# One kernel, four places reordered: split stores, key weights and their loads, the routed experts' first tiles, and the turning of the queries' rows

## The reference

```python
x = x + mlstm(layernorm(x), ctx, ctx)          # 16 heads of 32, gates, decay matrix, normalised per head
x = x + moe(layernorm(x))                      # rms norm, 8 experts, top 2, silu(gate) * up, down; + a shared expert
x = x + xattn(layernorm(x), ctx)               # q, ki, vi: 16 heads of 128, q and k rms-normalised over 2048 columns
x = x + x @ ternary(weight).T + bias
# xattn, cut:
k_img = rms_norm(img_ctx @ ki_w + ki_b, nki_s) # ki_w 512 x 2048
v_img = img_ctx @ vi_w + vi_b
out = (softmax(q @ k_img.T / sqrt(128)) @ v_img) @ o_w + o_b
```

## Time and profile before

| | us |
|---|---|
| median of 3 runs (1359.07 to 1367.22) | 1366.83 |
| the profiled execution | 1370.19 |
| its span in the profile | 1368.5 |
| values and gates | 0 to 197 |
| heads and keys | 197 to 475 |
| routed experts | 569 to 781 |
| queries | 781 to 1003 |

### The profile page before, as it was taken

One profiled execution on the slowest core, in us unless ns is written; L12 is line 12 of the kernel. 1 busy time (PEld: TensorE's weight loads), 2 busy tenths in 40 slices (PEclk: granted clock), 3 DMA queues, 4 the chain that ended last, 5 costly groups with the idle time before them and its releaser, 6 DMA issues. The chain is left out here.

```text
span 1368.5 us, 24512 instructions
## 1 busy us (share of the span) xinstructions
PE 1298.8 (95%) x7390; PEld 1072.4 (78%) x7391; DVE 840.9 (61%) x1614; ACT 742.9 (54%) x1839; POOL 382.6 (28%) x358
## 2 busy tenths in 40 slices
PE   7998998989999899899989989999989999999998
PEld 6786876767776768688876678888878888888887
DVE  3644546767679774444444377635477777777865
ACT  4334538786777351345455545544676555556651
POOL 0111014273719006399331153036000000000041
PEclk9999999999999899999999999999999999999999
DMA  7847799877787194675648787473565555555403
GB/s 250 307 186 266 265 319 311 267 252 244 258 254 231 63 333 183 204 218 156 201 147 269 265 256 214 137 232 132 185 202 161 162 158 165 159 168 155 122 32 123
DMA packets 168183, 280.99 MB, mean 205 GB/s; under 512 B 29920, under 2 KB 58336, under 8 KB 167840
## 3 DMA queue, kind: packets, MB, share of 16 engines
q1 hardware_dynamic: 142288, 224.44, 51.6%
q0 software_dynamic: 8672, 29.37, 6.6%
q10 hardware_dynamic: 17136, 26.09, 5.2%
HBM read 171.04 MB, written 108.80 MB: 204 GB/s over the span
## 5 line engine op out<-in xcount | busy, mean ns | idle before, releaser
L120 PE MATMUL banks<-of_shared_split,key_lead 128*128 128x512 f32 x256 | 110.0, 430 | 17.5 <-DVE key_trail L1392 10.7
L2973 ACT ACTIVATE prob<-banks,attend_row,rq 128x128 f32<-128x128 f32 x248 | 110.4, 470 | 0.0
L2986 ACT ACTIVATE attend_ol<-banks,of_attend_vbias 128x512 fp32r<-128x512 f32 x64 | 44.2, 691 | 116.9 <-PE banks L3185 116.9
L120 PE MATMUL banks<-wo,attend_ol 128*128 (+1 forms) x256 | 106.3, 415 | 0.0
L121 PE MATMUL banks<-of_shared_split,key_lead 128*128 128x512 f32 x256 | 104.9, 410 | 0.0
L122 PE MATMUL banks<-of_shared_split,key_trail 128*128 128x512 f32 x256 | 104.8, 410 | 0.0
L120 PE MATMUL banks<-queries_rows_split,queries_wl 128*128 128x512 f32 x256 | 100.9, 394 | 0.0
L122 PE MATMUL banks<-wo,attend_ot 128*128 (+1 forms) x256 | 100.8, 394 | 0.0
L121 PE MATMUL banks<-wo,attend_ol 128*128 (+1 forms) x256 | 100.0, 391 | 0.0
L122 PE MATMUL banks<-queries_rows_split,queries_wt 128*128 128x512 f32 x256 | 99.9, 390 | 0.0
L121 PE MATMUL banks<-queries_rows_split,queries_wl 128*128 128x512 f32 x256 | 99.8, 390 | 0.0
(11 more groups left out here) (399 smaller groups left out, 3569.5 us busy)
## 6 DMA issues: line engine op xcount, KB each, us to landing
mlstm_gmax<-running_max SPq DMA_DIRECT2D x36, 512.0 KB, 5.8
k_heads<-heads_key ACTq DMA_DIRECT2D x64, 256.0 KB, 4.5
q_heads<-queries_head SPq DMA_DIRECT2D x64, 256.0 KB, 2.7
q_ahead<-q_heads SPq DMA_DIRECT2D x64, 256.0 KB, 4.2
of_attend_k<-k_heads SPq DMA_DIRECT2D x60, 256.0 KB, 4.0
of_attend_v<-v_heads SPq DMA_DIRECT2D x60, 256.0 KB, 3.3
key_raw<-in_L_xattn_ki_w SPq DMA_DIRECT2D x20, 512.0 KB, 5.4
sorted_rows<-of_shared_split SPq DMA_DIRECT2D x2, 5120.0 KB, 28.6
```

The lines of the kernel that those rows point to most:

```text
L120: nc.tensor.matmul(out, lead_l, lead_r, start=first, stop=False)
L2973: ins = nc.scalar.activation(prob[:, j % 2, b, :], ps[:, j % 2, b * S:(b + 1) * S], ACT.Exp, bias=row[:, j % 2, 1, b:b + 1], scale=rq[:, b ...
L2986: nc.scalar.activation(ol[:, par, j, :], ps[:, 4 + j % 2, :], ACT.Identity, bias=vbias[:, bass.ds(quad_of(it) * 4 + j, 1)]).then_inc(ol_do ...
```

## The change

In values and gates, the eight stores of the split context are issued at units 21, 22, 25 and 26 instead of 30, 32, 34 and 36, and the load of the third quarter of x comes at unit 8, behind a store of values, instead of 7.

In heads and keys, the inner pairs of `KEYS` alternate between groups for each head rather than each pair of heads; the weights of a visit are formed one unit earlier where its predecessor in the same buffer allows it (`SPLIT_AT`, `FORMED`); SyncE issues the eight split loads ahead of the other work of its step; and the tail's instructions are put in another order on ScalarE and VectorE.

In routed experts, the leads and trails of the second tile precede the cut of the second expert's weights, and the inputs of the first two down products are split ahead of the last gate.

In queries, `staged` counts batches, and TensorE turns the first group batch by batch.

```diff
--- before.py
+++ after.py
@@ -194,7 +194,8 @@
         TRAILS = {OPENS[q + 1] - (6 if q < QUADS - 2 else 5) + c: (q + 1, c) for q in range(QUADS - 1) for c in range(C)}
         STATS, NORMS = 8, 16
         GATES = [20 + (UNITS - 13 - 20) // 3 * g for g in range(G)]
-        TOKENS = {4: 0, 5: 1, 7: 2, 9: 3}
+        TOKENS = {4: 0, 5: 1, 8: 2, 9: 3}
+        SPLITS = {21: 0, 22: 1, 25: 2, 26: 3}
         TURN = len(FOURS) % 2
         AHEAD_AT = (OPENS[-2] + 2, OPENS[-2] + 4)
         stage = [A.kT[:].rearrange("p c n -> p (c n)").rearrange("p (b d) -> p b d", b=GB), A.ctx[:]]
@@ -291,11 +292,11 @@
                 if u % 4 == 0 and u:
                     store_four(u // 4 - 1)
                 if u in TOKENS:
-                    if u > 4:
+                    if u % 4:
                         sp.wait_ge(product, u - 1)
                     load_x(TOKENS[u])
-                if u % 2 == 0 and 30 <= u < 30 + 2 * G:
-                    g = (u - 30) // 2
+                if u in SPLITS:
+                    g = SPLITS[u]
                     sp.wait_ge(trail_done, (g + 1) * C)
                     for k, t in ((0, lead), (1, trail)):
                         sp.dma_start(split_dram[k, :, :, g * N:(g + 1) * N].rearrange("c p t -> p c t"),
@@ -712,11 +713,16 @@
     UNITS = PER * G
     HALF = PER // 2
     KEYS = [(k % 2 * HALF + 2 * p + j, g, k * HALF + 2 * p + j)
-            for k in range(G + 1) for p in range(HALF // 2) for g in (k - 1, k) if 0 <= g < G for j in range(2)]
+            for k in range(G + 1) for p in range(HALF // 2)
+            for g, j in ([(g, j) for g in (k - 1, k) for j in range(2)] if p in (0, HALF // 2 - 1) else
+                         [(g, j) for j in range(2) for g in (k - 1, k)]) if 0 <= g < G]
     VISITS = HALF * (G + 1)
     KEY_BANKS = (6, 7, 1)
     FIRST_OF = [min(u for u, key in enumerate(KEYS) if key[2] == v) for v in range(VISITS)]
     LAST_OF = [max(u for u, key in enumerate(KEYS) if key[2] == v) for v in range(VISITS)]
+    SPLIT_AT = [0, 0] + [max(LAST_OF[v - 2] + 2, FIRST_OF[v] - 1) for v in range(2, VISITS)]
+    FORMED = dict((SPLIT_AT[v], v) for v in range(2, VISITS))
+    assert len(FORMED) == VISITS - 2
     OPENS = [min(u for u, key in enumerate(KEYS) if key[1] == g) for g in range(G)]
     CLOSES = [max(u for u, key in enumerate(KEYS) if key[1] == g) for g in range(G)]
     with Phase(nc, "heads") as ph:
@@ -825,13 +831,17 @@
 
             def next_raw(g, m):
                 u = unit_number(g, m)
-                v = KEYS[u][2]
-                if u == FIRST_OF[v] and v % 2 and v // 2 + 2 < VISITS // 2:
+                v = FORMED[u] if u in FORMED else u if u < 2 else 0
+                if v % 2 and v // 2 + 2 < VISITS // 2:
                     sp.wait_ge(wt_done, v + 1)
                     A.load_raw(sp, (v // 2 + 2) % (PER // 2))
 
             def body(g, first, last=False):
                 for n in range(PER):
+                    if not first and not last and n == PER - 2 - LAG:
+                        sp.wait_ge(product, CLOSES[g - 1] + 1)
+                        for part in range(2 * C):
+                            A.load_split(sp, g + 1, part)
                     if n % 2 == 0:
                         k = n // 2
                         sp.wait_ge(dec_done, g * PER + n + 2)
@@ -858,10 +868,6 @@
                         load_ctx(g + 2, n - PER + GB)
                     if first and LAG <= n < LAG + 2 * C:
                         A.load_split(sp, 1, n - LAG)
-                    if not first and not last and n == PER - 2 - LAG:
-                        sp.wait_ge(product, CLOSES[g - 1] + 1)
-                        for part in range(2 * C):
-                            A.load_split(sp, g + 1, part)
                     if n == LAG and last:
                         sp.wait_ge(A.v_stored, 16 * ((H1 // 4 * G - len(DEFERRED)) // 2))
                         for w, at in zip(E1.weights, (0, C * F, 2 * C * F)):
@@ -1028,10 +1034,10 @@
 
             def weight_lead(g, m):
                 u = unit_number(g, m)
-                v = KEYS[u][2]
-                if u == FIRST_OF[v] and v >= 2:
+                if u in FORMED:
+                    v = FORMED[u]
                     act.wait_ge(product, LAST_OF[v - 2] + 1)
-                    A.weight_lead(act, KEYS[u][0], v // 4)
+                    A.weight_lead(act, KEYS[FIRST_OF[v]][0], v // 4)
 
             def keep_key(g, m):
                 u = unit_number(g, m)
@@ -1072,12 +1078,14 @@
             for g in range(1, G):
                 body(g, False)
             last = G - 1
-            row_sums(last)
             for m in range(PER - LAG, PER + 1):
-                if m + 1 < PER:
+                if m < PER - LAG + 2:
                     weight_lead(last, m + 1)
                 keep_key(last, m - 1)
+                if m == PER - LAG:
+                    row_sums(last)
                 if m == PER - LAG + 1:
+                    weight_lead(last, m + 2)
                     square(last, 0)
                     square(last, 1)
                     act.wait_ge(early_agg, 1)
@@ -1176,9 +1184,9 @@
 
             def weight_trail(g, m):
                 u = unit_number(g, m)
-                v = KEYS[u][2]
-                if v >= 2 and u == FIRST_OF[v]:
-                    A.weight_trail(dve, v, KEYS[u][0])
+                if u in FORMED:
+                    v = FORMED[u]
+                    A.weight_trail(dve, v, KEYS[FIRST_OF[v]][0])
 
             def add_square(g, m):
                 dve.wait_ge(ksq_done, unit_number(g, m) + 1)
@@ -1235,18 +1243,19 @@
                     weight_trail(last, m + 1)
                 add_square(last, m - 1)
 
+            finish(PER - LAG)
             quad(last, QUADS - 1)
             divisor(last)
+            finish(PER - LAG + 1)
             close(last, 0)
             close(last, 1)
-            finish(PER - LAG)
-            finish(PER - LAG + 1)
+            weight_trail(last, PER - LAG + 3)
             dve.wait_ge(row_stats.summed, EARLY)
             for b in range(EARLY):
                 ins = nc.vector.bn_aggr(K.mv[:, b, :], K.stats[:, b, :])
             ins.then_inc(early_agg, 1)
             variance(last, 0)
-            finish(PER - LAG + 2)
+            add_square(last, PER - LAG + 1)
             variance(last, 1)
             dve.wait_ge(early_root, 1)
             early = slice(0, EARLY)
@@ -1321,7 +1330,7 @@
                     pe.wait_ge(ksq_done, u - 2)
                 part = lambda k, c: split[:, of % 2, k, c, :]
                 for c in range(C):
-                    ins = three_passes(nc, ps[:, KEY_BANKS[u % 3], :], wl[:, m % 2, c, :], wt[:, m % 2, c, :], part(0, c),
+                    ins = three_passes(nc, ps[:, KEY_BANKS[u % 3], :], wl[:, v % 2, c, :], wt[:, v % 2, c, :], part(0, c),
                                        part(1, c), c == 0, c == C - 1)
                 ins.then_inc(product, 1)
 
@@ -2092,7 +2101,7 @@
                               ).then_inc(hidT_stored[par], 16)
 
             def slot(t):
-                if counts(t, 1):
+                if counts(t, 2):
                     lead_of(t)
                 if counts(t, 1) and not counts(t, 2):
                     cut_gate_up(2)
@@ -2103,17 +2112,6 @@
                 if counts(t, 1):
                     silu(move(t, -1))
 
-            act.wait_ge(raw_loaded[0], 32)
-            cut_piece(0)
-            lead_of((0, 0))
-            for c in range(1, C):
-                cut_piece(c)
-            cut_gate_up(1)
-            slots(act, slot)
-            store_hidden(move(LAST, -2))
-            keep_hidden(move(LAST, -1))
-            silu(LAST)
-            store_hidden(move(LAST, -1))
             def hidden_lead(t):
                 n, m = tile_of(t), t[1]
                 act.wait_ge(ring_loaded[m], t[0] * 16 + 16)
@@ -2123,6 +2121,20 @@
                 nc.scalar.activation(hl[:, m % 2].rearrange("p f s -> p (f s)"), ring[m], ACT.Copy
                                      ).then_inc(hl_done, 1)
 
+            act.wait_ge(raw_loaded[0], 32)
+            cut_piece(0)
+            lead_of((0, 0))
+            for c in range(1, C):
+                cut_piece(c)
+            lead_of((0, 1))
+            cut_gate_up(1)
+            slots(act, slot)
+            store_hidden(move(LAST, -2))
+            hidden_lead((0, 0))
+            hidden_lead((0, 1))
+            keep_hidden(move(LAST, -1))
+            silu(LAST)
+            store_hidden(move(LAST, -1))
             def keep(t):
                 n, m = tile_of(t), t[1]
                 act.wait_ge(down, n + 1)
@@ -2139,8 +2151,6 @@
                     keep_hidden(LAST)
                     store_hidden(LAST)
 
-            second_slot((0, 0))
-            second_slot((0, 1))
             act.wait_ge(gu, TILES)
             for e in range(4, E):
                 act.wait_ge(dn_loaded[e % 4], 32)
@@ -2203,11 +2213,12 @@
             trail_of((0, 0))
             for c in range(1, C):
```

(20 more changed lines are left out.)

## The result

The changed kernel takes 0.9943 of the time of the kernel before, 95% interval 0.9922 to 0.9963. The medians are 1359.3 us over 11 runs and 1366.4 us over 12; the ratio stands for 7.8 us less, between 5.1 and 10.7. One more run of the changed kernel, 1446.3 us at a mean granted clock of 0.84, was in a slower state of the chip and is left out. Forecast were 18 us less. The time lies inside the range that was given, but the gain is less than half of the forecast, and by the bound of 1% it is "the same" where "faster" was the likeliest.

What follows compares the result with a forecast made beforehand. TensorE, busy nearly throughout, was taken as the bound, through its waits and low clock. -4.9 - 13.4 + 1.0 + 1.3 + 0.2 - 2.4 = -18.2 us, from 1366.8 to about 1349 us; forecast's own range 1342 to 1356.

Steps and rivals of the forecast that it cites:

- the range that was given: Whole kernel: 1340 to 1362 us, said to hold most of the forecast sum and late-masks cases, 0.8.
- the bound of 1%: Whole kernel: a time within 1%, 1353 to 1380 us, counts as the same; faster had 0.57, same 0.40.
- Values: Values, split stores issued earlier: the 3.25 us wait for x_lead and 1.7 us of low clock go; gain 4.9 us.
- Queries: Queries' first turns: staging batch by batch lets TensorE start and end earlier; gain 2.4 us, from 1.6 to 3.3.
- Heads: Heads, keys and split loads: short waits, two load waits and the clock behind them go; gain 13.4 us, 9 to 14.
- the short waits: Heads: three starts of an inner unit wait for the key trail, 0.5 to 0.8 us each; 2.1 us go.
- the masks come late: Heads: load_g lands behind the 2 MB of split loads, losing some 10 of 13.4 us; 1359 us, chance 0.28.
- The sign that the prediction gave for late masks: Heads: a growing TensorE wait for heads_dec or heads_cmat would show that the masks come late.
- The rival that the forming blocks ScalarE: Heads: earlier forming holds up exponentials, 1.5 us a visit cancelling the gain; at 2.2 us, 1375 us; chance 0.05.
- The tail: End of heads: the 4.01 us stall moves to about 6 us ahead of the sums; loss 1.0, between -1 and 3.
- its last add ends within about half a microsecond of where it did: Tail of heads, VectorE's last add into heads_total: 2.7 us of extra steps eat what the earlier products give.
- The routed part: Routed experts: waits return as some 3.8 us ahead of tile 2 and 4 at down; losses 1.3 and 0.2 us.

Runs made afterwards that it cites:

- an eighth of the bytes: The changed kernel, but for the last two groups each of the eight split loads brings 32 KB instead of 256 KB; ran once, 1356.6 us.
- the mended tail: Changed kernel without its routed part, ScalarE keeping unit 61 ahead of the squares, VectorE adding the last squares ahead of factor; 0.9856 of the kernel before, -19.7 us.

## Why the prediction was wrong

**Values** was right: 4.9 us forecast, 6.7 measured alone (3.7 to 9.6), 5.3 in both traces. **Queries** was right in size as far as can be told: 2.4 forecast, 1.9 alone, in an interval from 4.8 gained to 1.1 lost.

**Heads** was right in size by the times: the loads were sized at 3.84 + 2.74 + 4.7 = 11.3 us and gave 11.2 alone (7.5 to 15.0), the short waits at 2.1 and gave 1.9. The traces show less, and a cost that the sum put at nothing, the late key stores. Ahead of the tail the loads alone are 8.9 us ahead, and the changed kernel has 8.6 of the 13.4; at the first crossing it was 12.1 us ahead of the kernel before and gave 3.9 back. The rival "the masks come late" had the cause, the bytes ahead of load_g, but the wrong victim: the prediction looked at load_g's landing, which did come later (9.8 us after the issue in the median, where 5.8 were counted), and the wait came by the key stores. These go out on ScalarE's queue, and the prediction named nothing on that queue. The Trainium skill, "DMA: Bandwidth & Descriptors", section "Queues, rings and completion order", says that each DMA engine takes turns between the queues that have work for it. The trace agrees so far as the stores on one queue landed in 6.4 us (the median) instead of 4.4 while the other queue had more bytes to move; the turns themselves no trace shows.

The sign that the prediction gave for late masks came, waits for heads_cmat that grow from 3.0 to 4.9 us, but they are 5.5 us with an eighth of the bytes and 4.6 with the key order alone, so they don't show late masks. The rival that the forming blocks ScalarE falls: its waits for a product ahead of a lead fell from 33.4 us to 20.6.

**The tail** is the first step that failed. Its cost was taken as 1.0 us, between -1 and +3; it is 4.4 us alone (1.5 to 7.1). The step "its last add ends within about half a microsecond of where it did" was wrong. It ended at 463.5 us in the kernel with the tail alone, 1.7 us later than before. From 441.7 us to this add VectorE carries out the same operations in both kernels and idles no longer (3.2 us against 3.8). But four of them are slower in the new order, where the prediction counted each at its usual length: the first trail and add take 1.03 and 1.09 us instead of 0.69 and 0.68, and two small operations of the divisor 0.70 and 1.17 us instead of 0.23 and 0.20, together 2.2 us more. And the earlier products give nothing: ScalarE keeps unit 61 behind the squares of the heads, so VectorE idles 2.48 us for its squares, as it idled 2.52 us for a trail before. Timeline of VectorE, first in the kernel before, then with the tail alone:

```profile
442.78 0.23 DVE L1127 TENSOR_TENSOR heads_small<-heads_small,mlstm_nat 128x64 f32<-128x64 f32 x1 [0.39 <-ACT heads_small L1015]
443.04 0.20 DVE L1129 TENSOR_SCALAR heads_small<-heads_small 128x64 f32<-128x64 f32 x1
...
453.20 0.69 DVE L1392 TENSOR_TENSOR key_trail<-key_raw,key_lead 128x512 fp32r<-128x512 f32 x1 [2.52 <-ACT key_lead L1387]
```

```profile
441.78 1.03 DVE L1395 TENSOR_TENSOR key_trail<-key_raw,key_lead 128x512 fp32r<-128x512 f32 x1
442.74 1.09 DVE L1194 TENSOR_TENSOR heads_total<-heads_total,heads_ksq 128x512 f32<-128x512 f32 x1
...
444.82 0.70 DVE L1129 TENSOR_TENSOR heads_small<-heads_small,mlstm_nat 128x64 f32<-128x64 f32 x1 [0.39 <-ACT heads_small L1015]
445.56 1.17 DVE L1131 TENSOR_SCALAR heads_small<-heads_small 128x64 f32<-128x64 f32 x1
...
456.06 0.69 DVE L1194 TENSOR_TENSOR heads_total<-heads_total,heads_ksq 128x512 f32<-128x512 f32 x1 [2.48 <-ACT heads_ksq L1050]
```

All five kernels with the new or the mended tail have the two small operations at 0.7 and 1.17 us, and none of nine with the old tail is above 0.23 and 0.67, so they are slow with the new order and not by chance. In the kernel with the tail alone they end at 445.5 and 446.7 us, within 0.1 us of the ends of two operations of GpSimd; that these hold them up is not shown.

The clock took the other 2.0 of the 3.7 us. With the new tail the sums and the products behind them run wholly at the lower level; in the kernel before the sums began at the full clock, and it fell at 463.5 us. The 1.0 us that the prediction put on the whole step had no room for this. First the window of the sums' start in the kernel before, then one of the changed kernel from the start of its sums on, columns as in the earlier trace rows:

```profile
461.90:463.40 1.50, 1.50 (x14) 1.50 (x14) 1.50 (x1) 0.00 (x0) 0.00 (x0) 1.00 0.00 0
```

```profile
449.80:459.60 9.80, 9.79 (x39) 9.21 (x40) 7.74 (x13) 0.27 (x1) 0.00 (x0) 0.50 0.00 0
```

**The routed part** is the second. The waits were forecast nearly as they came: 3.8 us ahead of tile 2 were forecast and 3.36 came one step earlier, ahead of the turn of tile 0's hidden rows, for hidden(0) itself; some 4 at the third product and 4.41 came, half clock behind the first:

```profile
573.15 0.69 PE L2280 MATMUL banks<-ident,routed_hid 128*128 128x128 f32 x2 [3.36 <-DVE routed_hid L2191]
...
573.00:579.00 6.00, 5.85 (x17) 4.82 (x18) 2.68 (x10) 1.80 (x6) 5.92 (x6) 0.50 0.86 265
...
711.40 0.49 PE L120 MATMUL banks<-routed_w,routed_hl 128*128 x1 [4.41 <-DVE routed_ht L2199]
```

So here only the size can have been wrong. The sum put 1.5 us on it; alone it took 3.1 us (0.3 to 6.0), an interval that holds the 1.5. Together the two parts were sized at 2.5 us and cost 7.5 by the single kernels, 9.6 by the difference. Without them the change gives 17.4 us, and the forecast for the rest was 18.2 + 2.5 = 20.7, which the interval of 11.3 to 22.7 holds. Of the 10.4 us that are missing between 18.2 and 7.8, the difference puts 7.1 on the two parts and 3.3 on the rest.

**The clock was priced as if it were certain.** Each wait was charged the fall of the clock that followed it in the one profile of before. That profile was one of the more expensive ones: 1370.2 us, against a median of 1366.4. The same wait doesn't always bring the fall. First the kernel before at one of the early key units and the window behind it, then the kernel with the values part alone at the same unit (windows of TensorE alone, columns as in the earlier trace rows):

```profile
228.66 0.79 PE L120 MATMUL banks<-of_shared_split,key_lead 128*128 128x512 f32 x1 [1.72 <-DVE key_trail L1392]
...
228.00:235.00 7.00, 6.34 (x15) 0.52 0.90 325
```

```profile
225.51 0.50 PE L120 MATMUL banks<-of_shared_split,key_lead 128*128 128x512 f32 x1 [1.73 <-DVE key_trail L1393]
...
224.60:231.60 7.00, 4.86 (x20) 1.00 0.91 326
```

1.72 and 1.73 us of wait, granted clock 0.52 and 1.00. All fourteen traces have this wait, at 1.72 to 1.73 us: the lower level comes with it for 6.8 us in three of them, for 3.4 in eight and not at all in three. At the queries' turns the waits differ somewhat, and so does what follows: 3.74 us with 0.50 behind it before, 3.00 us and this in the kernel with values alone:

```profile
794.88 1.97 PE L2708 MATMUL banks<-ident,of_attend_raw 128*128 128x128 f32 x16 [3.00 <-DVE of_attend_raw L2606]
...
794.00:801.00 7.00, 6.12 (x35) 1.00 1.02 389
```

About 10 of the pair's 13.6 us are clock: the lower level lasts 45 us in the trace after and 65 in that of before, and half of the 20 us is lost work. TensorE's idle gaps (over 0.15 us each, without the one at the start) fell only from 56 to 54 us. This part differs from execution to execution by some microseconds, and the 7.8 us over many runs hold it as a mean.

The six parts alone add up to -14.2 us, and the whole change gives -7.8. With intervals of about 3 us on each this doesn't show that the parts spoil each other; whether they do stays open.

## What to carry to other kernels

When an order is changed to take a wait away, work through what the next consumer stands behind: a wait whose releaser stays where it was comes back one step later, and if the clock falls there over dense work it costs more than it did. Put the step's long pieces (a cut of 2 us, four multiplications) behind the small operations that TensorE waits for, or break them over several tiles: here two parts that lost 7.5 to 9.6 us became, so mended, 13 us faster than the order of before (30.4 against 17.4). And price the clock behind a wait by more than one profile: here the lower level lasted between 26 and 65 us in fourteen traces.

## What the runs showed of the hardware that was not expected

Loads on SyncE's queue delay stores on ScalarE's queue when the DMA engines are full: in the 25 us around the first crossing the stores landed in 6.4 us in the median and 8.3 at the longest at a share of 0.94 of the engines' time, and in 4.4 and 7.1 us when seven eighths of the split loads' bytes were left out. And a wait of the same length at the same place, 1.72 to 1.73 us, is followed by a granted clock of 0.5 in one execution and 1.0 in another.
